# A gather–compute–scatter kernel: each indirect DMA waits for one a few places ahead of it, and the tiles of a unit change their order

## The reference

```python
xs, xv = s @ W_up0, einsum(v, W_up1)            # per node
ss, vv = xs[senders], xv[senders]               # gather by src, which is random
w = mlp(radial_embedding(edge_length))          # 4 x 32 weights per edge
mid_s = concat([w0 * ss, w3 * (vv . Y1)])
mid_v = concat([w1 * ss * Y1, w2 * vv])
msg = segment_sum(mid, receivers)               # scatter-add by dst
out = layernorm(x + (msg_s @ W_out0, msg_v @ W_out1) / 16)
```

## Time and profile before

| | us |
|---|---|
| median of three timed runs | 1323.9 (1321.33 to 1324.72) |
| the profiled execution's own time | 1335.3 |
| its span, first to last instruction | 1333.5 |
| POOL busy in the span | 1014.3 (76%) |
| TensorE busy | 928.8 (70%) |
| VectorE busy | 692.2 (52%) |
| ScalarE busy | 537.5 (40%) |
| mean share of the 16 DMA engines that is busy, all queues | 47% |

### The profile page before, as it was taken

The page is one execution under the profiler, slowest core; times in us unless marked ns, Lnnn a source line. Parts: engine busy times, 40 slices in busy tenths (PEclk is TensorE's granted clock), DMA queues, the critical chain, the costliest instruction groups (busy, mean ns, idle before and its releaser), DMA issues.

```text
span 1333.5 us, 25760 instructions
## 1 busy us (share of the span) xinstructions
PE 928.8 (70%) x6206; PEld 871.6 (65%) x6206; DVE 692.2 (52%) x2882; ACT 537.5 (40%) x1403; POOL 1014.3 (76%) x817
## 2 busy tenths in 40 slices
PE   2577688787788867776876768777876766767800
PEld 1477577787677766766776767676776766767700
DVE  5364334465576456556556466465465556555402
ACT  5233233244445534444444444434443434534301
POOL 6347878888888888888888888888888888888761
PEclk7588877887888889889879897788788888898955
DMA  4377786433443443453453453443444444443332
GB/s 131 113 184 161 168 185 120 94 65 67 114 97 67 93 116 69 90 119 69 90 120 67 91 118 69 93 110 73 94 92 91 94 92 93 93 91 68 59 28 63
DMA packets 82548, 130.36 MB, mean 98 GB/s; under 512 B 16168, under 2 KB 66763, under 8 KB 81232
## 3 DMA queue, kind: packets, MB, share of 16 engines
q0 software_dynamic: 68992, 51.43, 28.7%
q1 hardware_dynamic: 12888, 77.27, 17.3%
q10 hardware_dynamic: 632, 1.29, 0.3%
HBM read 78.31 MB, written 77.22 MB: 117 GB/s over the span
## 4 chain that ended last, share of the span: by engine, by line
issue 31%; POOL 28%; DMA 11%; PE 8%; another core or an unknown queue 7%; SPq 5%; ACT 4%; POOLq 3%; ACTq 1%; DVE 0%; DVEq 0%
POOL acc L444 20%; POOL sender L420 7%; DMA acc<-msg,index 6%; DMA acc<-in_x_dram 5%; SPq L295 3%; PE ps_msg L553 2%; PE ps_sum L541 2%; ACT normed L693 2%; PE ps_wts L528 2%; POOLq L427 1%; PE ps_hid L512 1%; PE ps_dst L494 1%; PE ps_sT L500 1%; ACT hid L656 1%
## 5 line engine op out<-in xcount | busy, mean ns | idle before, releaser
L444 POOL DMA_INDIRECT acc<-msg,index x392 | 621.1, 1585 | 170.3 <-issue 111.0
L420 POOL DMA_INDIRECT sender<-in_x_dram,index x392 | 386.8, 987 | 123.5 <-issue 111.9
L541 PE MATMUL ps_sum<-same,mid 128*128 128x128 f32 x1568 | 248.0, 310 | 1.5 <-issue 0.8
L541 PEld LDWEIGHTS ps_sum<-same,mid 128*128 128x128 f32 x1568 | 240.3, 226 | 10.0 <-DVE mid L930 0.8
L915 DVE TENSOR_TENSOR wts<-ps_wts,bias 128x512 f32<-128x512 f32 x98 | 67.8, 692 | 323.2 <-PE ps_wts L528 205.4
L528 PE MATMUL ps_wts<-mlp,hid 128*128 128x128 f32 x784 | 139.4, 335 | 104.9 <-ACT hid L668 100.6
L632 ACT COPY sumT<-ps_sum 128x512 f32<-128x512 f32 x196 | 114.9, 587 | 235.5 <-remote 131.3
L553 PE MATMUL ps_msg<-outw,sumT 128*128 128x64 f32 x1568 | 202.0, 285 | 2.3 <-ACT sumT L632 1.6
L553 PEld LDWEIGHTS ps_msg<-outw,sumT 128*128 128x128 f32 x1568 | 200.0, 206 | 3.2 <-issue 1.2
L528 PEld LDWEIGHTS ps_wts<-mlp,hid 128*128 128x128 f32 x784 | 126.6, 245 | 111.8 <-ACT hid L668 107.0
L512 PE MATMUL ps_hid<-hid,mlp 128*128 128x256 f32 x196 | 78.8, 490 | 150.2 <-ACT hid L656 110.1
(11 more groups left out here) (135 smaller groups left out, 1061.5 us busy)
## 6 DMA issues: line engine op xcount, KB each, us to landing
acc<-in_x_dram SPq DMA_DIRECT2D x80, 312.5 KB
total<-acc SPq DMA_DIRECT2D x30, 832.0 KB
out_dram<-normed SPq DMA_DIRECT2D x29, 832.0 KB
sender<-in_x_dram,index POOLq DMA_INDIRECT x392
acc<-msg,index POOLq DMA_INDIRECT x392
out_dram<-normed ACTq DMA_DIRECT2D x1, 832.0 KB
vec_raw<-in_edge_attr_dram SPq DMA_DIRECT2D x1, 576.0 KB
acc<-zeros SPq DMA_DIRECT2D x1, 320.0 KB, 3.9
```

What stands on the lines that cost most here:

```text
L420: pool.indirect_dma_start(sender[:, u % SRING, i, :], None, x, bass.IndirectOffsetOnAxis(ap=index[:, u, 0, i:i + 1], axis=0)).then_inc(gat ...
L444: pool.indirect_dma_start(acc, bass.IndirectOffsetOnAxis(ap=index[:, v, 1, i:i + 1], axis=0), msg[:, v % RING, i, :], None, compute_op=ALU.add
L541: mm = pe.matmul(ps_sum[r][:, i, h, :], mid[:, b, 2 * r + i, P * h:P * (h + 1)], same[:, b, 2 * r + i, :], start=True, stop=True)
```

## The change

- The tiles' order in a unit becomes R's 0, R's 2, R''s 0, R''s 2 (`(r q)` for `(q r)` in `turns`).
- With n the number of a scatter counted over all units, scatter n waits until scatter n - 3 has landed. The nearer ones (n - 1, and for the first scatter of a unit n - 2 too) are waited for only where the unit's flag is set, in units 0 and 1 as well.
- The flag now says whether a tile of the unit overlaps the one or two tiles just ahead of it, over unit bounds, and no longer whether any two of the unit's four overlap.
- A gather waits for the fourth gather ahead of it (the same place in the unit ahead). Its semaphores become eight (`gathered[b][i]`); those of the first two units' gathers are the scatters' own, `slot_done`, which are the old `scattered` with counts 16 higher.
- TensorE waits for each of the four gathered tiles ahead of its transpose, where it waited once for all four. ScalarE and SyncE wait for the same landings as before under the new name.
- VectorE computes the flags over a flat row of 392 tiles (`meet` and `meet_too` change shape), and POOL clears `meet` first.

```diff
-            return a.rearrange("p (j w) (q r) -> p w q j r", w=2, r=2)[:, w]
+            return a.rearrange("p (j w) (r q) -> p w q j r", w=2, r=2)[:, w]
...
+            def landed(n):
+
+                return slot_done[n // G % 2][n % G], 16 * (n // G // 2) + 32
+
+            def here(u, i):
+
+                return (slot_done[u][i], 16) if u < 2 else (gathered[u % 2][i], 16 * (u // 2))
+
             def gathers(u):
 
-                if u >= 2:
-                    pool.wait_ge(gathered[u % 2], 16 * G * (u // 2))
                 if u >= SRING:
                     pool.wait_ge(senderT_ps, u - SRING + 1)
                 for i in range(G):
+                    if u >= 1:
+                        pool.wait_ge(*here(u - 1, i))
...
-                if v >= 1:
-                    for i in range(G):
-                        pool.wait_ge(scattered[1 - c][i], 16 * ((v + 1) // 2))
                 for i in range(G):
-                    if i >= 1:
-
-                        if v >= 2:
-                            pool.wait_ge(scattered[c][i - 1], 16 * (v // 2) + 16 * meets)
-                        else:
-                            pool.wait_ge(scattered[c][i - 1], 16)
+                    n = G * v + i
+                    if n >= 3:
+                        pool.wait_ge(*landed(n - 3))
+                    for of in (n - 2, n - 1) if i == 0 else (n - 1,):
+                        if of >= 0:
+
+                            to, count_after = landed(of)
+                            pool.wait_ge(to, count_after - 16 + 16 * meets)
...
-                pe.wait_ge(gathered[b], u * (16 * G // 2) + 16 * G - 16 * G * b // 2)
                 if k >= 1:
                     pe.wait_ge(senderT_ready, u)
                 for i in range(G):
+                    if k < 2:
+                        pe.wait_ge(slot_done[b][i], 16)
+                    else:
+                        pe.wait_ge(gathered[b][i], 8 * (u - b))
...
+                for apart in range(1, 3):
+                    n = TILES - apart
+                    dve.tensor_tensor(meet[:, apart - 1, apart:TILES], hi[:, 0:n], lo[:, apart:TILES], ALU.is_ge)
+                    mm = dve.tensor_tensor(meet_too[:, apart - 1, apart:TILES], hi[:, apart:TILES], lo[:, 0:n], ALU.is_ge)
```

More of the change, by code:

```diff
@@ L113, in bass_gnn @@
         high = sb("high", [1, UNITS, G])
-        meet = sb("meet", [1, UNITS, G * (G - 1) // 2])
-        meet_too = sb("meet_too", [1, UNITS, G * (G - 1) // 2])
+        meet = sb("meet", [1, 2, TILES])
+        meet_too = sb("meet_too", [1, 2, TILES])
         piece_int = sb("piece_int", [1, UNITS], I32)
@@ L208, in bass_gnn @@
         sp_passed = sem("sp_passed")
-        gathered = [sem(f"gathered{b}") for b in range(2)]
+        gathered = [[sem(f"gathered{b}_{i}") for i in range(G)] for b in range(2)]
         basis_staged = sem("basis_staged")
@@ L234, in bass_gnn @@
         msg_ready = sem("msg_ready")
-        scattered = [[sem(f"scattered{b}_{i}") for i in range(G)] for b in range(2)]
+        slot_done = [[sem(f"slot_done{b}_{i}") for i in range(G)] for b in range(2)]
         total_in = [sem(f"total_in{b}") for b in range(2)]
@@ L337, in landed @@
                 for i in range(G):
-                    sp.wait_ge(scattered[1][i], 16 * j + 16)
+                    sp.wait_ge(slot_done[1][i], 16 * j + 32)
             def store(h, b):
@@ L401, in _ @@
             pool.memset(dense_orders[:, :], 0)
+            pool.memset(meet[:, :, :], 0.0)
             for a in least:
@@ L419, in gathers @@
                 for i in range(G):
+                    if u >= 1:
+                        pool.wait_ge(*here(u - 1, i))
                     pool.indirect_dma_start(sender[:, u % SRING, i, :], None, x,
                                             bass.IndirectOffsetOnAxis(ap=index[:, u, 0, i:i + 1], axis=0)
-                                            ).then_inc(gathered[u % 2], 16)
+                                            ).then_inc(here(u, i)[0], 16)
             def scatters(v):
-                c = v % 2
                 order = pool.value_load(scatter_orders[0:1, v:v + 1], min_val=2, max_val=2 * PIECES - 1)
@@ L445, in scatters @@
                                             msg[:, v % RING, i, :], None, compute_op=ALU.add
-                                            ).then_inc(scattered[c][i], 16)
+                                            ).then_inc(slot_done[v % 2][i], 16)
             pool.wait_ge(index_in, 1)
@@ L639, in msg_out @@
                     for i in range(G):
[L640 removed]
+                        act.wait_ge(slot_done[b][i], 8 * (v - b) - 8 * RING + 32)
                 act.copy(msg[:, slot, :, 0:MUL].rearrange("p s i k -> p (s i) k"), ps_msg[:, :, 0:MUL])
@@ L801, in make_scatter_orders @@
             def make_scatter_orders():
[L803 to L808, removed]
-                link(mm)
-                link(dve.tensor_tensor(meet[:, :, :], meet[:, :, :], meet_too[:, :, :], ALU.mult))
-                link(dve.tensor_reduce(meet_unit[:, :], meet[:, :, :], AX_X, ALU.max))
+                lo, hi = (a[:, :, :].rearrange("p v i -> p (v i)") for a in (low, high))
+                for apart in range(1, 3):
+                    n = TILES - apart
+                    dve.tensor_tensor(meet[:, apart - 1, apart:TILES], hi[:, 0:n], lo[:, apart:TILES], ALU.is_ge)
+                    mm = dve.tensor_tensor(meet_too[:, apart - 1, apart:TILES], hi[:, apart:TILES], lo[:, 0:n], ALU.is_ge)
+                link(mm)
+                for apart in range(1, 3):
+                    mm = dve.tensor_tensor(meet[:, apart - 1, apart:TILES], meet[:, apart - 1, apart:TILES],
+                                           meet_too[:, apart - 1, apart:TILES], ALU.mult)
+                link(mm)
+                link(dve.tensor_tensor(meet[:, 0, :], meet[:, 0, :], meet[:, 1, :], ALU.max))
+                link(dve.tensor_reduce(meet_unit[:, :], meet[:, 0, :].rearrange("p (v i) -> p v i", i=G), AX_X, ALU.max))
                 link(dve.tensor_reduce(pieces[:, :], high[:, :, :], AX_X, ALU.max))
```

## The result

The changed kernel takes 1289.56 us in the median of 4 runs (1286.99 to 1291.72); the kernel before, timed beside it, takes 1323.8 (1321.33 to 1324.72, 4 runs). The ratio is 0.9743, 95% interval 0.9721 to 0.9766: 34.2 us saved. The profiled execution of the changed kernel took 1289.87 us, with a span of 1288.1. That is 45.4 us under the span profiled of before, 11 more than the medians are apart, and so the two traces can't be subtracted as they stand; the experiments show where they differ.

The account below looks back on a forecast made before the run. POOL was taken as the bound, without a gap in the middle, with needless landing waits at both ends. Tail 13.5 + start 16.0 - fixed wait 1.0 = 28.5 us saved: 1323.9 to 1295.4, written 1295.5; range 1291 to 1305.

Parts of the forecast that it names:

- The tail: Behind the last gather, six POOL waits for the preceding unit's last scatter, 15.3 us, fall to gaps of 0.30: 13.5 us saved.
- The gathers and their waits that have passed: Three more gather waits per unit on POOL, already passed when reached, cost nothing; 15 us slower at the outside.
- The flags: In the new tile order no tile overlaps the one or two just ahead, so no unit's flag is set.
- The fixed wait under the copies: Fourth scatters waiting for the first: 0.1 us in each of about ten early units, 1.0 us lost; bounds 0 and 8.
- The start: Units 0 and 1: six waits for the scatter just ahead, 19.0 us, become gaps; 17.1 us possible, 16.0 if messages keep their times.
- The term that the prediction took off for the messages: POOL's least lead over messages, 17.0 us at unit 9, less 0.96 needed, limits the start's gain to 16.0 of 17.1 us.
- Carrying the difference over: Timed median is 11.4 us under the profiled execution; the same difference was assumed after the change, from 1306.8 to 1295.4.
- the messages that take the start's gain: Rival, chance 0.16: POOL waits for messages from unit 2 on; all 16.0 gone gives 1310.4 us, half gone 1302.4.
- the rule weighed in the prediction: A scatter's landing would also wait for SyncE's copies and stores; at the upper bound it costs 8, sum 21.5 us.

Follow-up runs that it names:

- r4_before: The kernel before, unchanged, run again on the fourth group's chip, which had no remote waits: 1325.06 us in one run.
- r4_after: The changed kernel, unchanged, on the fourth group's chip, which had no remote waits: 1289.1 us, ratio 0.9747 to the kernel before.
- e6: The kernel before, but its first scatter waits for four messages instead of one: 1362.75 us, ratio 1.0202 to the kernel before.
- e7: The changed kernel, but its first scatter waits for four messages instead of one: 1331.09 us, ratio 0.9966 to the kernel before.
- r3_before: The kernel before, unchanged, run again on the third group's chip, with remote waits: 1337.95 us in one run.
- r3_after: The changed kernel, unchanged, on the third group's chip, with remote waits: 1311.69 us, ratio 0.9821 to the kernel before.
- e4: The changed kernel, but each unit's first scatter waits for the last of the unit ahead, as before: 1329.84 us, ratio 0.9947 to the kernel before.
- r2_after: The changed kernel, unchanged, on the second group's chip, with remote waits: 1316.26 us, ratio 0.9854 to the kernel before.
- e1: The kernel before with only the gather half of the change; scatters and tile order as before: 1339.92 us, ratio 1.0002 to the kernel before.
- e5: The changed kernel with the old order of tiles in a unit, waits and flags as changed: 1490.41 us, ratio 1.1144 to the kernel before.
- e8: The kernel before with the first wait for four messages and a second copy beside each copy: 1360.0 us, ratio 1.0275 to the kernel before.
- e9: The changed kernel with the first wait for four messages and a second copy beside each copy: 1329.97 us, ratio 1.0045 to the kernel before.

## Why the prediction was wrong

Where the time went is read off the starts of the same scatters in two traces (us; a column is before minus after, and "r4" are r4_before and r4_after, "lead" e6 and e7, "r3" r3_before and r3_after):

| stretch | forecast | r4 | lead | r3 |
|---|---|---|---|---|
| to the first scatter | 0 | 2.2 | -0.4 | 1.0 |
| to unit 2 (the six waits) | 17.1 | 21.6 | 15.6 | 17.0 |
| unit 2 to 16 | -2.1 | -2.2 | -0.9 | -8.2 |
| unit 16 to 93 | 4.5 | 5.2 | 4.7 | 6.0 |
| unit 93 to the last scatter | 9.0 | 9.2 | 9.1 | 9.3 |
| to the end | 0 | -0.2 | 0.1 | 0.1 |
| sum | 28.5 | 35.8 | 28.3 | 25.2 |

(The forecast's 16.0 is 17.1 less 1.1 lost to the messages, and with the 1.0 for the fixed wait that is 2.1 from unit 2 on; its tail of 13.5 is six waits, two of which end ahead of unit 93. 19.0 less six gaps of 0.30 is 17.2, not 17.1.)

**The tail** was right: 13.5 said; in r4_before the six waits are 15.5 us, 13.7 over six gaps, and none is left in r4_after; 13.6 lie between e4 and r2_after. (28 scatters follow the last gather in both kernels, not 24.)

**The gathers and their waits that have passed** were right: nothing, within 2.3 us faster and 2.9 us slower (e1).

**The flags** were right: no flag is set in the new order, for in e7 no scatter behind the first has a gap over 0.4 us, and 174 us stand behind that (e5).

**The fixed wait under the copies** was right in kind, and small in size. It binds in the fourth scatters of several early units. In the trace of after, first to fourth scatter of unit 1 is 68.60 - 62.48 = 6.12 us where back to back it would be 5.67, and between the r4 traces 2.2 us were lost from unit 2 to 16, against 1.0 said. That the table's row comes out within 0.1 is luck: the forecast's other 1.1 there is a loss to the messages that did not occur. Said was also that no row passes the limit; in r4_before rows do (81.66 - 75.67 = 5.99 from a scatter's start to its dependant's in unit 1):

```profile
81.66 1.68 POOL L444 DMA_INDIRECT acc<-msg,index  x1 [4.37 <-DMA acc<-msg,index]
```

**The start** is the step that failed, as a size; that six waits become gaps was right. "Six waits of 19.0 us fall to six gaps" took the 19.0 from the one profiled execution, and "Nothing in the sum can save more than 30.6 (13.5 + 17.1)" made a bound of it. In r4_before, the one trace of before at the pace of the timed runs, the waits are 23.4. There 21.6 us instead of 17.1 are saved up to unit 2, 4.5 of the 7.3 by which that column passes the forecast. The length is no constant of the kernel: in the traces of before on the other chips the same six waits are 21.2, 19.4 and 19.5 us. More copies in flight lengthen them (e8), but in r4_before no more are in flight than in the trace, so why they are longest there stays open. On the chips with late results the start came out as forecast: POOL's first scatter of unit 2 starts at 93.84 and 94.50 in r2_after and r3_after, said was 94.

The term that the prediction took off for the messages, 1.1 us, was not due either: message 2 is ready at 74.6 in r4_before and POOL starts unit 2 at 99.6, 25 us of lead, where the prediction read 18.0. Another 2.2 us lie ahead of the first scatter, where the sum had nothing: message 0 is ready at 51.26 in r4_before and at 48.75 in r4_after. That need not be the change's, for e8, which has the waits of before, has it at 48.85; no run settles it.

**Carrying the difference over** is the assumption behind it. "The median of the timed runs is 11.4 us under that execution; I carry the same difference over" treats it as outside the sum. Part of it was inside. From the trace of before to r4_before, the first scatter comes 16.1 us sooner (68.34, 52.23), the stretch of the six waits is 4.9 us longer (42.4, 47.3), and the rest 1.0 longer: together the 10.2 us between their spans. From r3_before to r4_before it is 17.2 sooner and 4.3 longer, together the 12.9 between the spans. The first part is the late first message, which both kernels have on such chips, and cancels in the difference; the second is the change's to save.

**The rival** of the messages that take the start's gain (0.16) is what happens on the chips with late results, where the changed kernel saves 20.2 and 24.0 us instead of 34 or 35. In r3_after 8.2 us are lost from unit 2 to 16, most of them ahead of three first scatters, and with the lead 0.9. The forecast time of that rival, half gone, stood 7 us above the predicted time; on those chips the saving is 4.5 to 8.3 under 28.5. In the trace of the result, as in r4_after, no unit's first scatter after unit 0 has a gap over 0.31 us: the rival did not apply there.

## What to carry to other kernels

A wait for the last transfer, where the next doesn't depend on it, costs what is left of the landing each time that nothing else fills the engine. Here that was at the two ends of a loop and not in the middle, and its price was start to start less that of scatters back to back (4.13 - 1.87 = 2.3 us each in the tail). Before a sum is made from one profiled execution, ask which of its terms the gap between that execution and the median belongs to; here the gap, 11.4 us, was a third of what the change saved. And where a stretch lies under a bulk transfer, take the length of its waits as a range: the same six were 17.4 to 23.4 us with two copies in flight, and 28.1 with four.

## What the hardware showed

Two things were not expected. On three of four chips, each used at one time, VectorE and ScalarE took up TensorE's results late, in waits the profile calls remote (166.3 us in 63 waits, longest 17.1, at one line of r2_after), and early on the copies ran slower: in the second slice of the page, 33 to 66 us, 107 to 115 GB/s moved for the two kernels, against 192 and 191 on the fourth chip. The same kernel takes 1336 to 1338 us there and 1324 here. What holds them up was not found, nor whether the slow copies and the late results have one cause.

And the landing of a scatter of 128 rows depends on the traffic beside it. From start to the start of one that waits for it, it is 4.13 us without copies, 57.81 - 52.23 = 5.58, 5.10 and 5.51 in unit 0 with two copies in flight (r4_before), and 6.27, 6.64 and 6.93 with four (e8). To the third behind it is 102.58 - 95.44 = 7.14 in e9, with four, where back to back would be 5.67. This leans the way of the rule weighed in the prediction (the Trainium skill, "DMA: Bandwidth & Descriptors", section "Queues, rings and completion order"), that a semaphore increment lands only after every earlier write of that DMA engine. The trace agrees in that landings get longer under SyncE's copies, but no run here tells that order from plain sharing of the engines. With two copies in flight the fixed wait cost 2.2 us, not the 8 that the prediction had as its upper bound.
